# W between the two batches' contexts, stage one of tiles 4 to 7 inside the second layer, two adds on GpSimd

## What is computed

```python
q1 = fake_quant(layernorm(x)); q2 = fake_quant(ctx)      # to 0..255 and back
x1 = x + q1 @ q2                                         # layer one, ctx of the tile's batch
y = layernorm(x1)
logits = y @ W_router.T                                  # 8 experts, softmax over the top 2
lora = sum over experts of gate * (y @ A.T) @ B.T * 2    # rank 16 each
out = x1 + y @ W.T + bias + lora
```

## Time and profile before

| | us |
|---|---|
| median of 3 runs (lowest, highest) | 189.27 (189.17, 189.36) |
| span of the profiled execution, first to last instruction | 187.8 |
| TensorE busy | 164.8 (88%) |
| VectorE busy | 127.8 (68%) |
| ScalarE busy | 75.0 (40%) |
| GpSimd busy | 37.8 (20%) |

### The profile page before, as it was taken

The page is one execution under the profiler, slowest core; times in us unless marked ns, Lnnn a source line. Parts: engine busy times, 40 slices in busy tenths (PEclk is TensorE's granted clock), DMA queues, the critical chain, the costliest instruction groups (busy, mean ns, idle before and its releaser), DMA issues.

```text
span 187.8 us, 2573 instructions
## 1 busy us (share of the span) xinstructions
PE 164.8 (88%) x946; PEld 88.2 (47%) x946; DVE 127.8 (68%) x284; ACT 75.0 (40%) x100; POOL 37.8 (20%) x110
## 2 busy tenths in 40 slices
PE   6639997894697969369999999999999999999992
PEld 3323443351263427126556556556556556556541
DVE  6996577899666995995872872872882882831821
ACT  3476393997285923545124124124124124120000
POOL 8804504045500000080031031031021021000000
PEclk9975999999789999999999999999999999999999
DMA  5999999999300000000200200200200200200211
GB/s 116 401 417 410 409 408 407 409 409 411 127 5 0 0 0 0 0 0 3 112 2 3 112 0 0 112 3 0 112 0 3 112 0 0 108 7 0 105 65 56
DMA packets 6780, 22.74 MB, mean 121 GB/s; under 512 B 880, under 2 KB 1136, under 8 KB 6768
## 3 DMA queue, kind: packets, MB, share of 16 engines
q1 hardware_dynamic: 6624, 22.58, 30.8%
q10 hardware_dynamic: 144, 0.00, 0.0%
HBM read 18.38 MB, written 4.19 MB: 120 GB/s over the span
## 4 chain that ended last, share of the span: by engine, by line
PE 66%; DVE 28%; issue 3%; POOL 1%; DVEq 0%; POOLq 0%
PE ps L753 39%; PE ps L713 8%; PE ps L743 6%; DVE w_lo L522 4%; PE ps L722 3%; DVE xs L468 3%; PE ps L735 2%; PE ps L734 2%; PE ps L736 2%; DVE a L595 2%; DVE xs L417 2%; DVE a L454 2%; DVE bnx L427 2%; DVE bnx L425 2%; DVE a_t L461 1%
## 5 line engine op out<-in xcount | busy, mean ns | idle before, releaser
L753 PE MATMUL ps<-w_hi,yt_hi 128*128 128x512 f16 x128 | 39.5, 380 | 6.0 <-DVE w_lo L522 6.0
L713 PE MATMUL ps<-a,a_t 128*128 128x512 f16 x128 | 34.6, 407 | 6.9 <-DVE a_t L461 6.8
L753 PE MATMUL ps<-w_hi,yt_lo 128*128 128x512 f16 x128 | 39.4, 379 | 0.0
L753 PE MATMUL ps<-w_lo,yt_hi 128*128 128x512 f16 x128 | 39.4, 379 | 0.0
L287 ACT ACTIVATE a<-stage,prm,inv_s 128x1024 uint8<-128x1024 f32 x16 | 19.6, 1240 | 12.0 <-DMA stage<-in_ctx_kv 11.7
L713 PEld LDWEIGHTS ps<-a,a_t 128*128 128x128 f16 x128 | 12.4, 103 | 23.6 <-DVE a_t L461 10.2
L550 DVE MAX8 top<-ps 128x8 f32<-128x8 f32 x8 | 1.4, 175 | 30.6 <-PE ps L736 30.6
L235 POOL TENSOR_SCALAR root<-mvy 128x1 f32<-128x1 f32 (+1 forms) x7 | 2.9, 413 | 87.9 <-DVE mvy L421 87.9
L337 ACT ACTIVATE y<-xs,y_bias,y_scale 128x1024 f32<-128x1024 f32 x8 | 9.9, 1239 | 26.5 <-POOL y_bias L258 26.4
L753 PEld LDWEIGHTS ps<-w_hi,yt_hi 128*128 128x128 f16 x128 | 11.4, 98 | 18.3 <-DVE w_lo L522 7.7
L753 PEld LDWEIGHTS ps<-w_hi,yt_lo 128*128 128x128 f16 x128 | 12.5, 98 | 15.1
(11 more groups left out here) (127 smaller groups left out, 266.7 us busy)
## 6 DMA issues: line engine op xcount, KB each, us to landing
stage<-in_ctx_kv SPq DMA_DIRECT2D x16, 512.0 KB, 13.5
stage<-in_w_t SPq DMA_DIRECT2D x8, 512.0 KB, 11.8
xs<-in_x SPq DMA_DIRECT2D x7, 512.0 KB, 13.5
out_dram<-xs SPq DMA_DIRECT2D x7, 512.0 KB, 2.7
ar_raw<-in_ar_t SPq DMA_DIRECT2D x1, 544.0 KB, 15.9
xs<-in_x SPq DMA_DIRECT2D x2, 256.0 KB, 3.7
b_raw<-in_b_t SPq DMA_DIRECT2D x1, 512.0 KB, 11.2
bias_sb<-in_bias SPq DMA_DIRECT2D x1, 512.0 KB, 12.0
```

The source lines that it names most:

```text
L713: last = nc.tensor.matmul(ps[:, s1_bank(t) + h, :], a1_t[:, t % 4, k, :], a2[:, n, h * H:(h + 1) * H], start=k == 0, stop=k == K - 1)
L753: ins = nc.tensor.matmul(ps[:, OUT_BANK[p] + h, :], part, rhs[:, k, h * H:(h + 1) * H], start=k == 0 and part is hi and rhs is w_hi, stop= ...
```

## The change

- SP loads ar and W right behind ctx of batch 0, into the same eight buffers, then x4, B, bias, x5 to x7; ctx of batch 1 comes last, each load waiting for the w_lo that frees its buffer.
- ScalarE takes W's peaks two tiles at a time; ar and W get their scales in one go, from one matmul inside stage one of tile 3.
- Layer two of tiles 0 and 1 runs in two passes: first both products with w_hi, later the one with w_lo, with narrow between. Column sums of batch 1 follow at the end of tile 1; they write the PSUM banks that y's transposes use.
- Stage one of tiles 4 to 7 stands inside layer two of tiles 2 to 5, and the x work that belongs to it moves along on VectorE and GpSimd.
- On GpSimd now: `make_y` of tiles 0 and 1 (one operation of 1024 columns), `add_corr` of tiles 2 to 7 (an add of two tensors of 1024 columns), `add_bias` (a one-column step, a 1024-column operation that adds the row term, an add of two tensors of 1024 columns). ScalarE keeps y of tiles 2 to 7, VectorE the corr of tiles 0 and 1.
- hc's transpose lies in the columns of A's result, for tile 1 in a bank of its own; `gate_tile` waits for the transpose of the hc before.
- Ten more matmuls without use stand between the first column sums (`KEEP_WARM = (2, 5, 3)`), and the f16 identity is made earlier.

The diff's core, dedented, without the removed lines (the functions above hold them); in order SP, GpSimd, ScalarE, VectorE, TensorE:

```diff
+def load_ctx(n):
+    if n >= K:
+        sp.wait_ge(w_lo_ready, n - K + 1)
+    sp.dma_start(stage[:, n % RING, :], ctx_tiles[n]).then_inc(stage_in[n % RING], 16)
+def load_w(k):
+    sp.wait_ge(ctx_ready, k + 1)
+    sp.dma_start(stage[:, k, :], w_tiles[k]).then_inc(stage_in[k], 16)
...
+load_ctx(7)
+sp.dma_start(ar_raw[:, :, :].rearrange("p k c -> p (k c)"), ar_t).then_inc(ar_in, 16)
+for k in range(K):
+    load_w(k)
 load_x(4)
+sp.dma_start(b_raw[:, :], b_t).then_inc(b_in, 16)
+sp.dma_start(bias_sb[:, :], bias.partition_broadcast(P)).then_inc(bias_in, 16)
...
 load_x(5)
...
 load_x(6)
...
+for n in range(K, N):
+    load_ctx(n)
...
+def add_corr(t):
+    pool.wait_ge(x1_summed, t + 1)
+    pool.wait_ge(corr_ready, t // TB + 1)
+    nc.gpsimd.tensor_tensor(xs[:, t, :], xs[:, t, :], corr[:, t // TB, :],
+                            ALU.add).then_inc(x1_pool_ready, 1)
+def add_bias(t):
+    pool.wait_ge(rows_summed, t + 1)
+    then(nc.gpsimd.tensor_scalar(row_term[:, t:t + 1], rowsum[:, t:t + 1], row_shift, row_scale,
+                                 ALU.add, ALU.mult))
+    pool.wait_ge(y_ready, t + 1)
+    pool.wait_ge(bias_in, 16)
+    then(nc.gpsimd.tensor_scalar(xs[:, t, :], xs[:, t, :], 1.0, row_term[:, t:t + 1], ALU.mult, ALU.add))
+    nc.gpsimd.tensor_tensor(xs[:, t, :], xs[:, t, :], bias_sb[:, :], ALU.add).then_inc(bias_added, 1)
...
 scale_x(2, 4)
...
+scale_y(0)
+make_y(0)
+scale_y(1)
+make_y(1)
+add_corr(2)
+add_corr(3)
+scale_y(2)
+add_bias(0)
+scale_x(4, 5)
+scale_y(3)
+add_bias(1)
 for t in range(2, T):
...
+    if 3 <= t < T - 1:
+        scale_y(t + 1)
+    add_bias(t)
+    if t + 3 < T:
+        scale_x(t + 3, t + 4)
+    if t + 2 < T:
+        add_corr(t + 2)
...
+peaks_ar()
...
 make_corr(0)
...
+for i in range(K // 2):
+    peak_of_two_w(i)
+split_first_yt()
+for k in range(K):
+    split_w(k)
+split_yt(1)
+split_ar()
+split_b()
+for n in range(K, K + 6):
     quantise_ctx(n)
+gate_weight(0)
+for n in range(K + 6, N):
+    quantise_ctx(n)
+split_hct(0)
+make_y(2)
+gate_weight(1)
+sum_row(0)
+split_yt(2)
+split_hct(1)
 make_corr(1)
...
 sum_row(1)
...
+for t in range(2, T):
+    gate_weight(t)
     if t + 1 < T:
         make_y(t + 1)
...
+    sum_row(t)
     split_hct(t)
     if t + 1 < T:
         split_yt(t + 1)
...
+add_corr(0)
+statistics_y(0)
 quantise_x(3)
...
 sum_x1(1)
 take_a1t(3)
+sum_x1(2)
+spread_peaks()
+make_scales()
+split_first_yt()
+add_corr(1)
+statistics_y(1)
+sum_x1(3)
+for k in range(4):
+    split_w(k)
+split_yt(1)
+split_ar()
+for k in range(4, K):
+    split_w(k)
+statistics_y(2)
+gate_tile(0)
+split_b()
+statistics_x(4)
+split_hct(0)
+statistics_y(3)
+gate_tile(1)
 quantise_x(4)
...
+split_yt(2)
+split_hct(1)
+sum_out(0)
+for t in range(2, T):
     gate_tile(t)
+    if t + 2 < T:
+        take_a1t(t + 2)
     sum_out(t - 1)
+    if t + 3 < T:
+        statistics_x(t + 3)
+    if t + 2 < T:
+        sum_x1(t + 2)
     split_hct(t)
...
+    if t + 3 < T:
+        quantise_x(t + 3)
+    if t + 1 < T:
+        split_yt(t + 1)
     if t + 2 < T:
         statistics_y(t + 2)
...
+def late_product(t):
+    pe.wait_ge(a1t_ready, t + 1)
+    pe.wait_ge(corr_ready, 2)
+    for k in range(K):
+        product(t, k)
...
 column_sums(0, 0)
+keep_warm(KEEP_WARM[0])
 column_sums(0, 1)
+keep_warm(KEEP_WARM[1])
 pe.wait_ge(ident16_ready, 1)
 transpose_a1(0)
 column_sums(0, 2)
...
+keep_warm(KEEP_WARM[2])
+for t in range(TB):
     pe.wait_ge(a1t_ready, t + 1)
     if t >= 2:
         pe.wait_ge(x1_summed, t - 1)
     for k in range(K):
...
+        if t == TB - 1 and k == 3:
+            pe.wait_ge(diag_ready, 3)
+            nc.tensor.matmul(ps[:, PEAK_BANK, 0:3 * P], ones_b[:, :],
+                             diag[:, :, :].rearrange("p g n -> p (g n)"),
+                             start=True, stop=True).then_inc(peaks_done, 1)
         product(t, k)
         if t == 0 and k >= 3:
             column_sums(0, k)
...
+        if t + 1 < TB and k == 4:
+            transpose_a1(t + 1)
+        if t == TB - 1 and k == 4:
             transpose_y(0)
...
 for k in range(K):
+    pe.wait_ge(w_hi_ready, k + 1)
+    if k == 0:
+        pe.wait_ge(first_half_lo, 1)
     if k == K // 2:
         pe.wait_ge(yt_lo_ready, 1)
+    wide(0, k, False, parts=(0, 2))
+transpose_y(1)
+pe.wait_ge(x1_summed, TB)
+pe.wait_ge(yt_lo_ready, 2)
+for k in range(K):
+    wide(1, k, False, parts=(0, 2))
+pe.wait_ge(ar_lo_ready, 2)
+narrow(0)
+for k in range(K):
     pe.wait_ge(w_lo_ready, k + 1)
...
+    wide(0, k, False, parts=(1,))
+narrow(1)
+transpose_hc(0)
+for k in range(K):
+    wide(1, k, False, parts=(1,))
     if k == 4:
...
+        pe.wait_ge(b_lo_ready, 1)
+        lora(0, stop=True)
     if k == 6:
...
+        transpose_y(2)
+transpose_hc(1)
+pe.wait_ge(yt_lo_ready, 3)
+for k in range(K):
+    column_sums(1, k)
+lora(1, stop=True)
+for t in range(2, T - 1):
     pe.wait_ge(yt_lo_ready, t + 1)
     narrow(t)
...
+    pe.wait_ge(out_summed, t - 1)
     for k in range(K):
         wide(t, k, k == K - 1)
...
+        if k == 0 and t + 2 < T:
+            transpose_a1(t + 2)
+        if k == 2 and t + 2 < T:
+            late_product(t + 2)
+        if k == 3:
             transpose_hc(t)
...
+        if k == 4:
+            if t + 2 < T:
+                pe.wait_ge(x1_summed, t + 3)
             transpose_y(t + 1)
         if k == 5:
             lora(t)
```

More of the change, by code:

```diff
@@ L41, in xattn_ffn @@
     WARM_UP = 24
+    KEEP_WARM = (2, 5, 3)
     RING = 8
@@ L250, in scale_x, with scale_y @@
                                         ALU.add).then_inc(x_scaled, last - first)
-            def scale_y(first, last):
-                w = slice(first, last)
-                pool.wait_ge(y_measured, last)
+            def scale_y(t):
+                w = slice(t, t + 1)
+                pool.wait_ge(y_measured, t + 1)
                 inverse = inverse_roots(mvy, w)
@@ L484, in peaks_ar, with spread_peaks @@
[L484 to L493, removed]
+            def spread_peaks():
+                dve.wait_ge(peaks_act, PEAKS)
+                then(nc.vector.tensor_reduce(top_w[:, :], peak[:, 2:PEAKS], AX.X, ALU.max))
+                for i, peaks in enumerate((peak[:, 0:1], peak[:, 1:2], top_w[:, :])):
+                    nc.vector.tensor_scalar(diag[:, i, :], ident16[:, :], peaks, None, ALU.mult).then_inc(diag_ready, 1)
@@ L499, in split_ar @@
+                then(nc.vector.tensor_scalar(den_scale, power[:, 2:3], ratio, None, ALU.mult))
             def split_ar():
@@ L662, in _ @@
-            gate_tile(0)
-            split_w(5)
-            statistics_y(2)
-            split_w(6)
-            split_w(7)
-            split_b()
-            split_yt(1)
-            split_hct(0)
-            add_bias(0)
-            for t in range(1, T):
+            sum_x1(2)
[7 more added lines that the diff above has]
+                split_w(k)
@@ L691, in _, with keep_warm @@
         def _(pe):
+            def keep_warm(n):
+                for _ in range(n):
+                    nc.tensor.matmul(ps[:, WARM_BANK, 0:3 * P], ones16[:, 0:P], ones16[:, :], start=True, stop=True)
             def transpose_a1(t):
                 pe.wait_ge(x_quantised, t + 1)
-                if t >= 2:
-                    pe.wait_ge(a1t_ready, t - 1)
+                if t == TB:
+                    pe.wait_ge(x1_summed, TB)
+                elif t >= 2:
+                    pe.wait_ge(a1t_ready, t - 1 if t < TB else t)
                 bank = ps[:, a1_bank(t), :].bitcast(F16)
@@ L746, in lora, with wide @@
                     ins.then_inc(out_done, 1)
-            def wide(t, k, stop, halves=range(NH)):
+            def wide(t, k, stop, halves=range(NH), parts=(0, 1, 2)):
                 p = t % 2
                 hi, lo = yt_hi[:, p, k, :], yt_lo[:, p, k, :]
-                for part, rhs in ((hi, w_hi), (hi, w_lo), (lo, w_hi)):
+                every = ((hi, w_hi), (hi, w_lo), (lo, w_hi))
+                for i in parts:
+                    part, rhs = every[i]
                     for h in halves:
                         ins = nc.tensor.matmul(ps[:, OUT_BANK[p] + h, :], part, rhs[:, k, h * H:(h + 1) * H],
-                                               start=k == 0 and part is hi and rhs is w_hi, stop=stop and part is lo)
+                                               start=k == 0 and i == 0, stop=stop and i == 2)
                 if stop:
@@ L765, in _ @@
             column_sums(0, 2)
-            for t in range(T):
+            keep_warm(KEEP_WARM[2])
+            for t in range(TB):
                 pe.wait_ge(a1t_ready, t + 1)
```

270 lines of the change are left out of this document (74 added, 196 removed).

## The result

| | before | after |
|---|---|---|
| median | 189.26 us (4 runs, 189.17 to 189.36) | 197.74 us (4 runs, 197.51 to 198.42) |
| ratio | | 1.0457, 95% interval 1.0438 to 1.0477 |
| profiled execution: time, span, mean granted clock | time not known, 187.8, 0.973 | 197.51, 195.3, 0.953 |
| narrow(2) starts | 100.18 | 90.08 |

The change is slower, as forecast, by more than forecast: 8.5 us instead of 2.8. narrow(2) had to start before 84.5 for a gain; it starts at 90.08.

A forecast was written before the change was run, and what follows sets the result against it. TensorE's second layer runs at its own rate, so gains lie before it. narrow(2) at 86.2, plus 1.2 (clock) and 103.26, gives span 190.65; with 1.47, 192.1 us, 1.5% slower (190 to 193.8; full range 185.9 to 196).

The forecast's parts named there:

- The yardstick: Span is the start of narrow(2) plus 103.26; the change pays only if narrow(2) starts before 84.5.
- the walk: Following the queues of the changed kernel up to narrow(2), which it put at 86.2 before a further 1.2 for the clock.
- the scale: W's scale, after its last peak, reduction, diagonals and matmul: ready at 36.8, against 59.5 before.
- tile 0's hi pass: Tile 0's layer-two products with w_hi alone follow ScalarE and end at 47.65.
- the four blocked steps: Four one-column GpSimd steps of scale_y(1) go behind one VectorE w_lo each (1.19); scale_y(1) ends at 48.35.
- the long wait and its chain: Before tile 1's column sums TensorE idles 6.85 for yt_lo(2), behind quantise_x(4), scale_x(4), add_bias(0), sum_row(0) and tile 1's gate.
- rival (b): GpSimd's wide operations are dearer, 2.0 with one operand and 2.9 with two: 194.8; chance 0.17.
- The 1.47: Added to the forecast span: the trace's 187.8 stands 1.47 below the median of 189.27.
- What costs nothing: Tiles 2 to 5 last 18.07, GpSimd holding 11.6 per tile; keep-warm matmuls, identity cast and earlier transposes are absorbed.
- idle TensorE inside tiles 2 to 5: Named sign that the forecast is wrong; it expected tiles 2 to 5 of 18.1.
- the memset's row: GpSimd memset in the trace, 1.80 for 2048 columns, nearest basis for wide operations: 1.1 with one operand, 2.0 with two.
- (d): Rival: GpSimd or VectorE sets the pace of tiles 2 to 5, 2 us a tile, 200; chance 0.05.

The follow-up runs named there:

- e1: Changed kernel with one line moved: VectorE takes yt_lo(2) before quantise_x(4); 190.67 us, ratio 1.0084 to the kernel before.
- e2: Changed kernel with GpSimd doing scale_x(4) before add_bias(0), VectorE's order as changed; 190.51 us, ratio 1.0068 to the kernel before.
- e10: Changed kernel with scale_x(4) ahead of add_bias(0) on GpSimd and sum_row(1) ahead of make_corr(1) on ScalarE; 187.17 us, ratio 0.9867.
- e12: e9's kernel with gate_tile(0) ahead of quantise_x(4) and statistics of y(3) on VectorE, and 12 warm matmuls before the diagonals' wait; 183.75 us, ratio 0.9678.
- e8: Changed kernel, adds kept on GpSimd, with many orders mended together on VectorE, GpSimd and ScalarE, and warm matmuls at tile 1's waits; 188.33 us, ratio 0.9921.
- e6: Changed kernel with column-term and bias adds back on VectorE, the rest of the change kept; 188.93 us, ratio 0.9944 to the kernel before.
- e9: e6's adds on VectorE, plus seven w_lo after tile 1's split, statistics earlier, gate weight behind ctx 11, y(2) earlier, 13 warm matmuls; 187.32 us, ratio 0.9845.
- e5: Changed kernel with ScalarE summing the row of tile 1 ahead of the column term of batch 1; 195.62 us, ratio 1.0313 to the kernel before.
- e4: Changed kernel with 70 matmuls without use filling TensorE's waits at 48, 51 and 75 us; 194.06 us, ratio 1.0245 to the kernel before.

## Why the prediction was right in sign and wrong in size

**Right.** The yardstick and the walk: the scale at 36.90 (36.8), tile 0's hi pass to 47.75 (47.65), the four blocked steps, the long wait and its chain, 7.25 (6.85). That this wait makes 7 of the 8.5 us is shown by e1 and e2, that W's early start gains once the queues are reordered by e10 (adds on GpSimd) and e12 (adds on VectorE). The yardstick held to about 1 us: e1's profiled run, with narrow(2) at 84.21, took 190.21, e8's, at 83.76, took 189.16.

**Where 197.51 less 192.1 lies.** The time is above the range of the forecast (190 to 193.8) and above rival (b). narrow(2) came 2.7 after the forecast 87.4: hc(0) +1.5 (tile 1's first pass 53.91 for 52.85, transposes of y(1) at half clock, and a clock fall of 1.8 for 1.2), GpSimd's adds and steps +0.65 (the two-input add 2.34 for 2.0), column sums and lora +0.5 (7.81 for 4.84 + 2.5, the clock again). From narrow(2) to the end 105.2 for 103.26: +1.96. Outside the span 2.2 for 1.47: +0.75. Together 5.4. The 1.47 had set the span of one execution against the median of others: in the runs with both on record the kernel before stands 1.75 to 1.87 above its own span, e6, e9 and e12 1.76 to 1.94, and every kernel with the two adds on GpSimd 2.18 to 2.34. So about 0.3 of the 0.75 was a wrong term of the sum, and about 0.4 comes with the adds on GpSimd.

**The step that failed** is "What costs nothing": it took GpSimd's load of a steady tile, one add_bias with 6.5 us to spare, for tile 2. There add_bias(1) is due as well, because sum_row(1) is queued behind make_corr(1) on ScalarE (e5), and a wide GpSimd operation holds up VectorE's small gate steps. Put at nothing, this measured 1.85 of wait and 2.0 in the time of the tile; the prediction had named "idle TensorE inside tiles 2 to 5" as a sign of being wrong. I had reckoned that blocking as w_lo over GpSimd, and the other way for ar_lo alone (0.7), not for the gate. Nor for quantise_x, which from tile 2 on takes 2.83 instead of the 0.75 of the sum beside an add_corr, though no wait of TensorE came of that. The other terms had the right mechanism and were each too small. The wide operations cost 1.12 to 1.20 with one operand (1.1 taken) and 2.34 to 2.36 with two; the sum took 2.0 from the memset's row, and 2.1 with the gap behind it. The 2.25 worked out from the Trainium skill ("GPSIMD Engine Reference", section 3.1) was nearer; these runs put it 0.1 higher. None of this reaches the 194.8 of rival (b) by itself; (d), GpSimd pacing tiles 2 to 5, came true for tile 2 alone.

What stays open: why the time outside the span is 0.4 longer with the adds on GpSimd, and in which runs the clock falls at the first waits.

## What to carry to other kernels

Work moved to an idle engine is not free because that engine has room on average: list what is queued behind it there, and behind the engine that waits for it, at the one place where two such pieces fall together. Where GpSimd and VectorE share the tile's work, put VectorE work that the trace shows unharmed beside GpSimd's chains (here the statistics, and what reads PSUM), and the rest elsewhere; that it has a single input is not enough, as quantise_x shows below. An early start upstream pays only when every queue between it and its first user is reordered with it: with the same early start 8.5 us were lost in one arrangement, 2.4 won in another with the adds still on GpSimd (e10), and 5.7 with them on VectorE (e12).

## What the hardware showed that I had not expected

The blocking lengthens wide operations too, on both sides: make_y on GpSimd 4.32 instead of 1.20 beside four w_lo, ar_lo on VectorE 5.28 instead of 1.48 beside two GpSimd adds, a 128x8 VectorE step 1.96 instead of 0.29. VectorE's statistics did not do it: in the all-orders kernel GpSimd's steps kept their 0.19 beside them. But quantise_x, with one input, is hit as well: 2.83 beside add_corr in the changed kernel, 0.81 in e6, where the adds are on VectorE. GpSimd, then VectorE, in the changed kernel:

```profile
103.53 2.35 POOL L276 TENSOR_TENSOR xs<-xs,corr 128x1024 f32<-128x1024 f32 x1
```

```profile
103.60 2.83 DVE L492 TENSOR_SCALAR a<-xs,q_scale,q_bias 128x1024 uint8<-128x1024 f32 x1
```

The clock after the long wait came back only at 88.3 in the changed kernel's profile, 6.0 after work had resumed at 82.27, and from there to narrow(2) it took 7.81; after the same wait (7.22) in e5 it took 6.34, and 4.86 at full clock in e4. So one wait cost between 1.5 and 3.0. The wait at 35 left the clock at 1.00 in the changed kernel (2.72 long) and took it down (0.89 over 35 to 50) in e4 (2.37) and in e10 (2.31), whose instructions up to there are the same. The runs of the kernel before alone differ by up to 2.5 us, with different mean clocks (188.82 at 0.982, 191.33 at 0.964).
